# Top-k attention on one core: who negates the row maxima, and in which order TensorE takes scores, context and film products

## The chip, the cores and the metric

The kernel runs on one core of one Trainium2 chip. The metric is the device time of one execution in microseconds. Before the change it is 2488.77 us (median of 3 runs, 2488.7 to 2490.81). The engines are TensorE (PE, with its weight loads as PEld), VectorE (DVE), ScalarE (ACT), GpSimd (POOL) and SyncE (SP, which only issues transfers here). Each runs its own instruction list strictly in order, and semaphores tie the lists together.

## The reference, cut to what matters

The program is a decoder of two layers. The part that the change touches is the top-k attention of the second one, followed by an S4D convolution:

```
Q = (x_text @ Wq).reshape(B, T, H=4, DH=32);  K likewise from x_vision
scores = einsum('bthd,bghd->bhtg', Q, K) / sqrt(DH);  masked where vision_mask is false
topv, topi = top_k(scores, 32);  probs = softmax(topv)
attn = zeros.at[topi].set(probs);  attn_mean = attn.mean(axis=heads)
c_t = einsum('btg,bgd->btd', attn_mean, V) * text_mask
x = layernorm(x_text, g_norm_in, b_norm_in)
scale_in, shift_in   = split(c_t @ W_film_in  + b_film_in, 2)
x = x * (1 + gate * scale_in) + gate * shift_in
y = s4d(x, ...)
scale_out, shift_out = split(c_t @ W_film_out + b_film_out, 2)
y = y * (1 + gate * scale_out) + gate * shift_out
```

There are 2048 text rows, taken as 16 tiles of 128. A tile has 4 heads of 256 scores.

## The kernel before, in words

`topk_attention` (L2114 on) is one block with one hand-written instruction list for each engine. Nothing is scheduled automatically: the order of the Python calls is the order on the engine. Tile n goes through these steps.

- TensorE, `scores(n)`: four products of 32 rows (one a head) into the single buffer SC. ScalarE, `scale(n)`: copies SC to one of three buffers SS with the factor 1/sqrt(32). GpSimd, `mask(n)`: adds the mask to SS.
- VectorE: four rounds r = 0 to 3. Each finds the 8 greatest of each head (`max`, L2416) and strikes them out with `match_replace` (L2429), so that WW ends as the scores without the greatest 32. After round 0 `tensor_scalar` (L2435) writes NM, the negated maxima, and adds to `max_ready`. In round 0 of tile n stands also `inverse(n - 1)`: reciprocal and scaling of the sums of the tile before, which waits for `sums_ready`.
- ScalarE, in one turn n of its loop: `exp_left(n - 1)` (exp of WW), `diagonal(n - 1)` (four diagonal matrices of the inverse sums), `exp_all(n)` (exp of SS with the bias NM), `apply(n)` (layer norm of a row tile), `film(n - 2)` (copies out both film products), `turned_out(n - 1)`, `scale(n + 2)`, `pooled_out(n - 1)`, `sums(n)` (exp of the 32 found, with their sum).
- GpSimd: `selected(n)` subtracts WW from SS, which leaves only the 32 greatest, and adds to `probs_ready`.
- TensorE, `turn(n)`: multiplies SS by the diagonals, which turns the probabilities, weighs them and adds the heads up. `pool_context(n)`: the product with V. `film(n)`: two products of 512 columns with a bias row each, the first (in) and the second (out).

TensorE's loop before is, for one n: `scores(n + 2)`, `turn(n - 1)`, `pool_context(n - 1)`, `film(n - 1)` with both halves. At the stage's start it takes query groups 0 and 1, `scores(0)`, groups 2 and 3, `scores(1)`. VectorE first does the statistics of the layer norm of all 16 tiles, waits for the square root on ScalarE (`std_ready`), and then takes tile 0. The stage after this one (`s4d_convolve`) starts on TensorE once this block is finished.

Of the kernel before, what the change touches and what calls it, by code (L numbers as in the profile page):

```python
# [9 lines left out]
P = 128  # L10
B, S, D = 8, 256, 256
T = B * S
NT = T // P
KD = D // P
# [7 lines left out]
ALU = mybir.AluOpType  # L22
# [2097 lines left out]
def topk_attention(nc, io, X, XT, ident, CTT, Z, FO, conv_loads, inputs):  # L2120
# [5 lines left out]
    with Stage(nc, "tk") as st:  # L2126
# [37 lines left out]
        masked = st.sem("masked")  # L2164
        max_ready = st.sem("max_ready")
        found_ready = st.sem("found_ready")
# [16 lines left out]
        with st.block() as block:  # L2183
# [6 lines left out]
            def _(pe):  # L2190
# [36 lines left out]

                def film(n):
# [3 lines left out]
                    for i in range(2):  # L2232
                        if n:
                            pe.wait_ge(film_out_read if i else film_in_read, n)
                        for k in range(KD):
                            pe.matmul(FP[:, i, :], CTT[:, k, n * P:(n + 1) * P], WI[:, i, k, :], start=(k == 0), stop=False)  # L2236
                        add_bias(pe, ident, FP[:, i, :], BI[:, i, :]).then_inc(film_ready, 1)

                inputs.loads.wait(pe)
                queries(0)  # L2240
                queries(1)
                scores(0)
                queries(2)
                queries(3)
                scores(1)
                film_loads.wait(pe)
                for n in range(NT + 1):
                    if n + 2 < NT:
                        scores(n + 2)
                    if n:  # L2250
                        turn(n - 1)
                        pool_context(n - 1)
                        film(n - 1)

# [37 lines left out]
            def _(act):  # L2292
# [40 lines left out]
                def film(n):  # L2333
                    act.wait_ge(film_ready, 2 * n + 1)
                    if n >= 2:
                        act.wait_ge(updated, n - 1)
                    act.activation(FI[:, n % 2, 0:D], FP[:, 0, 0:D], ACT.Identity, scale=GATE[:], bias=ident[:, ONES:ONES + 1])
                    act.activation(FI[:, n % 2, D:2 * D], FP[:, 0, D:2 * D], ACT.Copy, scale=GATE[:]).then_inc(film_in_read, 1)
                    act.wait_ge(film_ready, 2 * n + 2)
                    act.activation(FO[:, n, :], FP[:, 1, :], ACT.Copy, scale=GATE[:]).then_inc(film_out_read, 1)  # L2340
# [8 lines left out]

                queries(0)  # L2350
                queries(1)
                scale(0)
                queries(2)
                queries(3)
                act.wait_ge(stats_ready, 1)
                act.activation(RS[:], MV[:, :, 1], ACT.Sqrt, bias=ident[:, EPS5:EPS5 + 1]).then_inc(std_ready, 1)
                scale(1)
                film_loads.wait(act)
                for n in range(NT + 2):
                    if 1 <= n <= NT:  # L2360
                        exp_left(n - 1)
                        diagonal(n - 1)
                    if n < NT:
                        exp_all(n)
                        apply(n)
                    if n >= 2:
                        film(n - 2)
                    if 1 <= n <= NT:
                        turned_out(n - 1)
                    if n + 2 < NT:  # L2370
                        scale(n + 2)
                    if 1 <= n <= NT:
                        pooled_out(n - 1)
                    if n < NT:
                        sums(n)

            @block.vector
            def _(v):
                ch = Chain(v, dve_chain)

                def norm_stats():
# [3 lines left out]
                    for t in range(NT):  # L2385
                        ins = v.bn_aggr(MV[:, t, :], raw[:, t, :])
                    ins.then_inc(stats_ready, 1)
                    v.wait_ge(stats_ready, 1)
                    v.wait_ge(std_ready, 1)
# [13 lines left out]
                for n in range(NT):  # L2403
# [5 lines left out]
                    for r in range(LAST + 1):  # L2409
                        src = ww if r else SS[:, n % RB]  # L2410
                        found = [0, 0]
                        for i, pair in enumerate(PAIRS):
                            if r:
                                ch.need(struck[i])
# [6 lines left out]
                        if r == 0 and n:  # L2421
                            inverse(n - 1)
                        for i, pair in enumerate(PAIRS):
                            if r == LAST and i:
# [5 lines left out]
                            if r == LAST and i:  # L2430
                                ins.then_inc(struck_ready, 1)
                            else:
# [923 lines left out]
```

## Time and profile before

| | us |
|---|---|
| median of 3 runs | 2488.77 |
| profiled execution, its own time | 2487.0 |
| its span | 2485.2 |
| TensorE busy, whole span | 2177.0 (88%) |
| VectorE busy, whole span | 1639.0 (66%) |
| ScalarE busy, whole span | 986.8 (40%) |
| first matmul of the top-k block | 1323.63 |
| VectorE's first search of a maximum | 1335.92 |
| first matmul of the convolution after it | 1557.14 |

So the block takes 233.5 us of the span. The shares of the whole program say little about it: other stages have other limits. In this block VectorE is busy nearly without a gap and TensorE has gaps in each tile, so the stage has to be read from the timeline of each engine, tile by tile. The execution's own time is 1.8 us above its span, and that goes with no stage.

### The profile page before, as it was taken

The numbers are of one execution on the slowest core, as the hardware profiler recorded it, in microseconds if no ns is written. First come the engines' busy times: TensorE is split into PE (matmuls) and PEld (weight loads), VectorE is DVE, ScalarE is ACT, GpSimd is POOL, SyncE is SP. The second block draws the span as 40 slices with busy tenths as digits, with TensorE's granted clock in tenths as the row PEclk, the third lists the DMA queues.
The fourth block names the chain that finished last, engine by engine and source line by source line (L and its number), as shares of the span: only waits on it lengthen the run. The fifth ranks groups of instructions, "written<-read, shape, count | busy, mean of one in ns | idle before, by whom it ended". The sixth has DMA issues, their size and how long they took to land. (4 is left out here: it accounts for less than half of the span.)

```text
span 2485.2 us, 34016 instructions
## 1 busy us (share of the span) xinstructions
PE 2177.0 (88%) x12318; PEld 1487.9 (60%) x12318; DVE 1639.0 (66%) x4179; ACT 986.8 (40%) x2077; POOL 889.1 (36%) x513
## 2 busy tenths in 40 slices
PE   8788888998996897699896888869888899999997
PEld 3355555633663897366474444336655788888886
DVE  6699999713656112546327997541479788888886
ACT  2498988512855331315424776032100312112210
POOL 0298888102532984214102655431401210111110
PEclk9899999999998899799998898979899999999998
DMA  3121111000005575300101000030030000000001
GB/s 102 44 81 47 51 48 51 2 11 0 1 1 193 207 239 174 101 1 2 58 0 41 1 1 1 1 117 0 1 136 1 3 1 1 1 1 1 1 1 34
DMA packets 63803, 109.34 MB, mean 44 GB/s; under 512 B 12498, under 2 KB 44115, under 8 KB 61973
## 3 DMA queue, kind: packets, MB, share of 16 engines
q1 hardware_dynamic: 62100, 102.98, 12.6%
q0 software_dynamic: 1536, 4.20, 0.5%
q8 instruction: 98, 1.61, 0.3%
q14 instruction: 69, 0.56, 0.1%
HBM read 94.19 MB, written 12.98 MB: 43 GB/s over the span
## 5 line engine op out<-in xcount | busy, mean ns | idle before, releaser
L749 POOL TENSOR_TENSOR XT<-mamba_DU,scan_BS 128x1024 f32<-128x1024 f32 x128 | 299.0, 2364 | 148.4 <-DMA scan_BS<-mamba_rows 110.8
L878 DVE TENSOR_TENSOR_SCAN scan_H<-scan_AB,XT 128x512 f32<-128x512 f32 x256 | 296.3, 1209 | 8.1 <-POOL XT L749 4.8
L3022 PE MATMUL ex_HP<-XT,pe_DOWN 128*128 128x256 f32 x1024 | 249.9, 391 | 6.3 <-PEq L2758 5.5
L3053 PE MATMUL ex_OP<-pe_UP,ex_GH 128*128 128x256 f32 x1024 | 231.5, 380 | 0.0
L3083 ACT ACTIVATE ex_GH<-ex_HP 128x512 f32<-128x512 f32 x128 | 76.4, 598 | 380.8 <-PE ex_HP L3022 346.1
L763 PEld LDWEIGHTS scan_TP<-ident,scan_H 128*128 128x128 f32 x1024 | 120.1, 142 | 157.2 <-DVE scan_H L878 81.2
L808 ACT ACTIVATE scan_AB<-mamba_E,mamba_AA 128x510 f32<-128x510 f32 x256 | 198.7, 776 | 37.9 <-DVE scan_H L878 33.5
L3022 PEld LDWEIGHTS ex_HP<-XT,pe_DOWN 128*128 128x128 f32 x1024 | 194.5, 195 | 31.9 <-issue 5.7
L3053 PEld LDWEIGHTS ex_OP<-pe_UP,ex_GH 128*128 128x128 f32 x1024 | 194.3, 190 | 25.9
L772 PE MATMUL scan_YT<-mamba_BC,ident 128*128 128x512 f32 x384 | 198.5, 599 | 4.1 <-ACT scan_YS L824 2.3
L763 PE MATMUL scan_TP<-ident,scan_H 128*128 128x128 f32 x1024 | 147.7, 278 | 45.8 <-DVE scan_H L878 45.8
L3109 POOL TENSOR_TENSOR ex_AS<-ex_AS,pe_IV 128x512 f16<-128x512 f16 x32 | 52.9, 1682 | 363.3 <-DVE ex_AS L3157 363.3
L3134 DVE TENSOR_TENSOR ex_L<-ex_IOTA,ex_KEYS 128x4096 f16<-128x4096 f16 x64 | 151.8, 2372 | 2.2
L817 ACT ACTIVATE mamba_BC<-scan_TP,scan_CT 128x512 f32<-128x512 f32 x192 | 129.3, 674 | 3.9 <-PE scan_TP L763 3.9
L3208 DVE SCALAR_TENSOR_TENSOR ex_GH<-ex_GP,ex_GH 128x1024 f32<-128x1024 f32 x64 | 78.4, 1225 | 61.0 <-issue 32.4
L1656 DVE TENSOR_SCALAR experts_HT<-experts_HP 128x320 f32<-128x320 f32 x32 | 15.7, 492 | 133.4 <-PE experts_HP L1593 133.4
L3042 PEld LDWEIGHTS ex_GP<-ex_R,ex_L 128*128 128x128 f16 x2048 | 77.8, 117 | 15.3 <-DVE ex_L L3134 4.5
L1608 PE MATMUL experts_YT<-experts_HT,moe_W 128*128 128x160 f32 x512 | 78.2, 314 | 8.0 <-ACT experts_HT L1624 7.5
L3042 PE MATMUL ex_GP<-ex_R,ex_L 128*128 128x32 f16 x2048 | 77.7, 191 | 7.2 <-DVE ex_L L3134 3.8
L2038 POOL TENSOR_TENSOR pfcore_A<-pfcore_A,pg_MASK 128x512 f32<-128x512 f32 x32 | 40.6, 1268 | 114.5 <-ACT pfcore_A L2018 114.5
L1608 PEld LDWEIGHTS experts_YT<-experts_HT,moe_W 128*128 128x128 f32 x512 | 74.7, 201 | 10.5 <-ACT experts_HT L1624 8.2
L2236 PE MATMUL tk_FP<-tk_WI,s_CTT 128*128 128x512 f32 x128 | 74.1, 708 | 7.6 <-ACT s_CTT L2348 7.6
(449 smaller groups left out, 4535.3 us busy)
## 6 DMA issues: line engine op xcount, KB each, us to landing
moe_W<-in_L_ffn_w SPq DMA_DIRECT2D x32, 1024.0 KB, 7.6
scan_BS<-mamba_rows SPq DMA_DIRECT2D x64, 256.0 KB, 3.2
pe_DOWN<-in_L_ffn_down SPq DMA_DIRECT2D x1, 4096.0 KB, 12.6
pe_UP<-in_L_ffn_up SPq DMA_DIRECT2D x1, 4096.0 KB, 22.7
moe_dispatch<-moe_BOTH SPq DMA_DIRECT2D x1, 2560.0 KB, 14.2
experts_XE<-moe_dispatch SPq DMA_DIRECT2D x16, 160.0 KB, 2.4
moe_answers<-experts_YE SPq DMA_DIRECT2D x16, 160.0 KB, 3.4
XT<-in_xT SPq DMA_DIRECT2D x4, 512.0 KB, 5.6
```

What stands on the lines that cost most here:

```text
L749: pool.tensor_tensor(BU[:, r % 2, cs], tokens(DU, cs, r // DS), row, ALU.mult).then_inc(bu_ready, 1)
L763: ins = pe.transpose(TP[:, i % SLOTS, c * P:(c + 1) * P], H[:, r % 2, c, tb * P:(tb + 1) * P], ident[:, 0:P])
L772: pe.matmul(YT[:, tb, :], ident[:, 0:P], HT[:, n % 4, :], start=(s == 0), stop=(s == DS - 1)).then_inc(y_added, 1)
L808: act.activation(later(AB[:, n % 2, :]), later(tokens(E, c, g)), ACT.Exp, scale=AA[:, 2 * c, s:s + 1], bias=AA[:, 2 * c, s:s + 1]).then_in ...
L817: act.activation(HT[:, n % 4, :], TP[:, item(r, tb) % SLOTS, :], ACT.Copy, scale=CT[:, TB * g + tb, s:s + 1]).then_inc(act_read, 1)
L878: v.tensor_tensor_scan(H[:, r % 2, c], AB[:, n % 2, :], BU[:, r % 2, c], 0.0, ALU.mult, ALU.add).then_inc(h_ready, 1)
L1608: ins = pe.matmul(YT[:, k * CAP:(k + 1) * CAP], W2[:, e % 2, c, k * P:(k + 1) * P], HT[:, e % 2, c, :], start=(c == 0), stop=(c == NHID - 1))
L3022: ins = pe.matmul(HP[:, n % 2, a, :], DOWN[:, k, 2 * q + a, :], XT[:, k, b * BLK:(b + 1) * BLK], start=(k == 0), stop=(k == KD - 1))
L3042: ins = pe.matmul(GP[:, n % 2, t, :], L[:, n % 2, t // RUN, :, t % RUN], R[:, n % 2, t // RUN, :, t % RUN], start=True, stop=True)
L3053: ins = pe.matmul(OP[:, m % 2, 0:D], GH[:, b % 2, j, a * P:(a + 1) * P], UP[:, j, :], start=(j == 0), stop=(j == J2 - 1))
L3134: v.tensor_tensor(L[:, n % 2], numbers(P), along(0, P), ALU.is_equal).then_inc(left_ready, 1)
L3208: v.scalar_tensor_tensor(gh, GP[:, n % 2].rearrange("p t j -> p j t"), 1.0 / PSCALE, gh, ALU.mult, ALU.mult).then_inc(gated, 1)
```

## The change

Three things change, all in `topk_attention`.

1. The negated maxima NM are made on ScalarE, at the head of `exp_all`, and not by VectorE. VectorE's last strike of round 0 now adds to `first_struck`; ScalarE waits for it, writes NM (128x4) with an activation, waits for its own write (`shift_ready`), and goes on with the exponentials.
2. At the start, `scores(0)` follows the first query group and `scores(1)` the third, and ScalarE's `scale(0)` and `scale(1)` move up with them. VectorE's reciprocal of the standard deviations moves from before tile 0 into round 1 of tile 0 (`norm_scale`).
3. In TensorE's loop the second film product of tile n - 2 stands between `turn(n - 1)` and `pool_context(n - 1)`, and `scores(n + 2)` behind `pool_context(n - 1)`; the first film product stays last. On ScalarE the copy of the second film product (`film_out`) moves behind `pooled_out(n - 1)`; `scale(n + 2)` stays in front of `pooled_out(n - 1)`.

```diff
+                def film(n, i):
                     pe.wait_ge(pooled_read, n + 1)
...
                 inputs.loads.wait(pe)
                 queries(0)
+                scores(0)
                 queries(1)
-                scores(0)
                 queries(2)
+                scores(1)
                 queries(3)
-                scores(1)
                 film_loads.wait(pe)
                 for n in range(NT + 1):
+                    if n:
+                        turn(n - 1)
+                    if n >= 2:
+                        film(n - 2, 1)
+                    if n:
+                        pool_context(n - 1)
                     if n + 2 < NT:
                         scores(n + 2)
                     if n:
-                        turn(n - 1)
-                        pool_context(n - 1)
-                        film(n - 1)
+                        film(n - 1, 0)
+                film(NT - 1, 1)
...
                 def exp_all(n):
-                    act.wait_ge(max_ready, n + 1)
+                    act.wait_ge(first_struck, n + 1)
+                    act.activation(NM[:, n % 2, :], MX[:, n % 2, :, 0], ACT.Copy, scale=-1.0).then_inc(shift_ready, 1)
+                    act.wait_ge(shift_ready, n + 1)
...
                         scale(n + 2)
                     if 1 <= n <= NT:
                         pooled_out(n - 1)
+                    if 2 <= n <= NT + 1:
+                        film_out(n - 2)
                     if n < NT:
                         sums(n)
...
                         if r == 0 and n:
                             inverse(n - 1)
+                        if r == 1 and n == 0:
+                            norm_scale()
...
-                        if r == 0:
-                            v.tensor_scalar(NM[:, n % 2, :], mx[:, :, 0], -1.0, None, ALU.mult).then_inc(max_ready, 1)
```

TensorE's list in the middle of the loop, before. tk_TP from tk_DG and tk_SS is `turn`, tk_TP from tk_AT and topk_V is `pool_context`, tk_FP with tk_WI and its row with tk_BI is one film product, tk_SC is `scores`:

```order
L2205 MATMUL tk_SC<-topk_KT,tk_QT 128x256 x4
L2216 MATMUL tk_TP<-tk_DG,tk_SS 128x128 x8
L2224 MATMUL tk_TP<-tk_AT,topk_V 128x128 x4
L2236 MATMUL tk_FP<-tk_WI,s_CTT 128x512 x2
L158 MATMUL tk_FP<-tk_BI,ident 128x512
L2236 MATMUL tk_FP<-tk_WI,s_CTT 128x512 x2
L158 MATMUL tk_FP<-tk_BI,ident 128x512
```

The same turn of the loop after the change:

```order
L2217 MATMUL tk_TP<-tk_DG,tk_SS 128x128 x8
L2236 MATMUL tk_FP<-tk_WI,s_CTT 128x512 x2
L158 MATMUL tk_FP<-tk_BI,ident 128x512
L2225 MATMUL tk_TP<-tk_AT,topk_V 128x128 x4
L2206 MATMUL tk_SC<-topk_KT,tk_QT 128x256 x4
L2236 MATMUL tk_FP<-tk_WI,s_CTT 128x512 x2
L158 MATMUL tk_FP<-tk_BI,ident 128x512
```

Between turning and context there was nothing, and now there is one film product; the scores stood ahead of the turning and now stand behind the context.

ScalarE's list in the middle of the loop, before. tk_AT is `turned_out`, tk_SS from tk_SC is `scale`, s_CTT is `pooled_out`, tk_FI and s_FO are the copies of the first and the second film product, tk_MJ is `sums`, tk_WW is `exp_left`:

```order
L2331 ACTIVATE s_Z<-X,tk_NB,tk_RS 128x256
L2337 ACTIVATE tk_FI<-tk_FP,ident,tk_GATE 128x256
L2338 ACTIVATE tk_FI<-tk_FP,tk_GATE 128x256
L2340 ACTIVATE s_FO<-tk_FP,tk_GATE 128x512
L2344 ACTIVATE tk_AT<-tk_TP 128x256
L2301 ACTIVATE tk_SS<-tk_SC 128x1024
L2348 ACTIVATE s_CTT<-tk_TP 128x2x128
L2311 ACTIVATE tk_MJ,tk_SM<-tk_MX,tk_NM 128x32 x4
L2317 ACTIVATE tk_WW<-tk_WW,tk_NM 128x256 x4
L2325 ACTIVATE tk_DG<-ident,tk_SM 128x128 x4
```

After the change:

```order
L2344 ACTIVATE tk_FI<-tk_FP,ident,tk_GATE 128x256
L2345 ACTIVATE tk_FI<-tk_FP,tk_GATE 128x256
L2353 ACTIVATE tk_AT<-tk_TP 128x256
L2306 ACTIVATE tk_SS<-tk_SC 128x1024
L2357 ACTIVATE s_CTT<-tk_TP 128x2x128
L2349 ACTIVATE s_FO<-tk_FP,tk_GATE 128x512
L2318 ACTIVATE tk_MJ,tk_SM<-tk_MX,tk_NM 128x32 x4
L2324 ACTIVATE tk_WW<-tk_WW,tk_NM 128x256 x4
L2332 ACTIVATE tk_DG<-ident,tk_SM 128x128 x4
L2310 ACTIVATE tk_NM<-tk_MX 128x4
```

The copy of the second film product moved from in front of tk_AT to behind s_CTT, and the write of tk_NM is new; the copy of the scores stands where it stood, one place ahead of s_CTT.

## Rows read from the trace of the kernel before

**Rows 1.** Windows: us, busy time (instructions) of PE, PEld, DVE, ACT, POOL, PEclk, DMA share, GB/s.

```profile
1340.00:1540.00 200.00, 159.26 (x638) 85.85 (x638) 199.48 (x799) 142.13 (x415) 110.52 (x91) 0.86 0.00 1
1391.00:1392.00 1.00, 1.00 (x8) 1.00 (x7) 1.00 (x5) 1.00 (x4) 0.86 (x2) 0.58 0.00 0
1400.00:1401.00 1.00, 1.00 (x2) 0.34 (x2) 0.97 (x6) 1.00 (x4) 0.08 (x1) 0.50 0.00 0
```

**Rows 2.** Timeline of VectorE, one tile: start us, us, instruction, [idle before it <-releaser].

```profile
1450.35 1.39 DVE L2416 MAX8 tk_MX<-tk_SS 128x8 f32<-128x256 f32 x4
...
1453.51 1.11 DVE L2435 TENSOR_SCALAR tk_NM<-tk_MX 128x4 f32<-128x4 f32 x1
1454.54 1.39 DVE L2416 MAX8 tk_MX<-tk_WW 128x8 f32<-128x256 f32 x4
...
1463.18 1.39 DVE L2416 MAX8 tk_MX<-tk_SS 128x8 f32<-128x256 f32 x4
```

**Rows 3.** Tile tk_NM: count, duration ns min/median/max, first and last start.

```profile
L2435 DVE TENSOR_SCALAR tk_NM<-tk_MX x16: 359/1110/1118, 1338.8 to 1530.5; 128x4 f32<-128x4 f32 x16
```

**Rows 4.** Timeline of GpSimd, the subtraction of the same tile.

```profile
1452.24 2.35 POOL L2270 TENSOR_TENSOR tk_SS<-tk_SS,tk_WW 128x1024 f32<-128x1024 f32 x1 [2.93 <-ACT tk_WW L2317]
```

**Rows 5.** Timeline of ScalarE, the same tile.

```profile
1450.46 1.70 ACT L2317 ACTIVATE tk_WW<-tk_WW,tk_NM 128x256 f32<-128x256 f32 x4 [0.24 <-DVE tk_WW L2429]
...
1454.66 1.71 ACT L2306 ACTIVATE tk_SS<-tk_SS,tk_NM 128x256 f32<-128x256 f32 x4 [1.32 <-DVE tk_NM L2435]
...
1457.57 0.67 ACT L2340 ACTIVATE s_FO<-tk_FP,tk_GATE 128x512 f32<-128x512 f32 x1
...
1458.40 1.02 ACT L2301 ACTIVATE tk_SS<-tk_SC 128x1024 f32<-128x1024 f32 x1
1459.90 0.38 ACT L2348 ACTIVATE s_CTT<-tk_TP 128x256 f32<-128x256 f32 x1 [0.48 <-PE tk_TP L2224]
1461.73 0.32 ACT L2311 ACTIVATE tk_MJ<-tk_MX,tk_NM 128x32 f32<-128x32 f32 x1 [1.44 <-DVE tk_MX L2416]
...
1462.87 0.19 ACT L2311 ACTIVATION_READ_ACCUMULATOR tk_MJ<-tk_MX,tk_NM 128x1 f32 x1
```

**Rows 6.** Timeline of TensorE, tiles in the middle and at the end.

```profile
1368.74 1.16 PE L2224 MATMUL tk_TP<-tk_AT,topk_V 128*128 128x128 f32 x8 [1.86 <-ACT tk_AT L2344]
1370.38 3.51 PE L2236 MATMUL tk_FP<-tk_WI,s_CTT 128*128 128x512 f32 x4 [0.47 <-ACT s_CTT L2348]
...
1454.65 2.05 PE L2216 MATMUL tk_TP<-tk_DG,tk_SS 128*128 128x128 f32 x16 [0.85 <-POOL tk_SS L2270]
...
1539.10 1.12 PE L158 MATMUL tk_FP<-tk_BI,ident 1*128 1x512 f32 x2
...
1542.07 1.12 PE L158 MATMUL tk_FP<-tk_BI,ident 1*128 1x512 f32 x2
1544.47 3.54 PE L2216 MATMUL tk_TP<-tk_DG,tk_SS 128*128 128x128 f32 x16 [1.28 <-POOL tk_SS L2270]
```

**Rows 7.** Timeline of TensorE, the first tiles.

```profile
1336.49 0.71 PE L2205 MATMUL tk_SC<-topk_KT,tk_QT 32*128 32x256 f32 x8 [1.24 <-ACT tk_SS L2301]
1343.79 1.24 PE L2205 MATMUL tk_SC<-topk_KT,tk_QT 32*128 32x256 f32 x8 [6.58 <-ACT tk_SS L2301]
1352.01 3.78 PE L2216 MATMUL tk_TP<-tk_DG,tk_SS 128*128 128x128 f32 x16 [6.99 <-POOL tk_SS L2270]
1356.26 1.51 PE L2224 MATMUL tk_TP<-tk_AT,topk_V 128*128 128x128 f32 x8 [0.47 <-ACT tk_AT L2344]
```

**Rows 8.** Timelines of ScalarE, GpSimd and VectorE, the stage's start.

```profile
1327.42 0.60 ACT L2295 ACTIVATE tk_QT<-tk_FP 128x512 f32<-128x512 f32 x1 [5.08 <-PE tk_FP L2195]
...
1331.04 1.02 ACT L2301 ACTIVATE tk_SS<-tk_SC 128x1024 f32<-128x1024 f32 x1
...
1332.22 2.35 POOL L2265 TENSOR_TENSOR tk_SS<-tk_SS,tk_MB 128x1024 f32<-128x1024 f32 x1 [8.18 <-ACT tk_SS L2301]
...
1335.92 1.40 DVE L2416 MAX8 tk_MX<-tk_SS 128x8 f32<-128x256 f32 x4
```

More of the change, by code:

```diff
@@ L2164, in topk_attention @@
         masked = st.sem("masked")
-        max_ready = st.sem("max_ready")
+        first_struck = st.sem("first_struck")
+        shift_ready = st.sem("shift_ready")
         found_ready = st.sem("found_ready")
@@ L2226, in pool_context @@
                     ins.then_inc(pooled, 1)
-                def film(n):
+                def film(n, i):
                     pe.wait_ge(pooled_read, n + 1)
@@ L2231, in film @@
                         pe.wait_ge(queries_read, T // G4)
[L2232 to L2237, printed above, removed]
+                    else:
+                        pe.wait_ge(film_out_read if i else film_in_read, n)
+                    for k in range(KD):
+                        pe.matmul(FP[:, i, :], CTT[:, k, n * P:(n + 1) * P], WI[:, i, k, :], start=(k == 0), stop=False)
+                    add_bias(pe, ident, FP[:, i, :], BI[:, i, :]).then_inc(film_ready, 1)
                 inputs.loads.wait(pe)
                 queries(0)
+                scores(0)
                 queries(1)
-                scores(0)
                 queries(2)
+                scores(1)
                 queries(3)
-                scores(1)
                 film_loads.wait(pe)
                 for n in range(NT + 1):
+                    if n:
[4 more added lines that the diff above has]
+                        pool_context(n - 1)
                     if n + 2 < NT:
@@ L2338, in film, with film_out @@
                     act.activation(FI[:, n % 2, D:2 * D], FP[:, 0, D:2 * D], ACT.Copy, scale=GATE[:]).then_inc(film_in_read, 1)
+                def film_out(n):
                     act.wait_ge(film_ready, 2 * n + 2)
@@ L2350, in _ @@
                 queries(0)
+                scale(0)
                 queries(1)
-                scale(0)
-                queries(2)
-                queries(3)
                 act.wait_ge(stats_ready, 1)
                 act.activation(RS[:], MV[:, :, 1], ACT.Sqrt, bias=ident[:, EPS5:EPS5 + 1]).then_inc(std_ready, 1)
+                queries(2)
                 scale(1)
+                queries(3)
                 film_loads.wait(act)
@@ L2387, in norm_stats, with norm_scale @@
                     ins.then_inc(stats_ready, 1)
+                def norm_scale():
                     v.wait_ge(stats_ready, 1)
@@ L2412, in _ @@
                         for i, pair in enumerate(PAIRS):
-                            if r:
+                            if r == 1 and i:
+                                v.wait_ge(first_struck, n + 1)
+                            elif r:
                                 ch.need(struck[i])
@@ L2431, in _ @@
                                 ins.then_inc(struck_ready, 1)
+                            elif r == 0 and i:
+                                ins.then_inc(first_struck, 1)
                             else:
                                 struck[i] = ch.mark(ins)
-                        if r == 0:
-                            v.tensor_scalar(NM[:, n % 2, :], mx[:, :, 0], -1.0, None, ALU.mult).then_inc(max_ready, 1)
                 inverse(NT - 1)
```

## The prediction, made before the changed kernel had run

> **What bounds the kernel now.** I read the windows first, then the timeline of each engine over one tile, last the tile of the negated maxima.
>
> The windows say who is full: in 200 us of the loop VectorE is busy for 199.48, TensorE for 159.26, ScalarE for 142.13, GpSimd for 110.52 [rows 1]. VectorE has no gap, so its work per tile is the period: from the first search of one tile to that of the next 1463.18 - 1450.35 = 12.83 us [rows 2]. The others wait for it: ScalarE stands idle 1.44 us before the sums and 1.32 us before the exponentials [rows 5].
>
> One VectorE row is odd. The write of NM has 4 elements a row and takes 1.11 us at the median, but 0.36 at least [rows 3]. In the tile shown it starts at 1453.51 and ends at 1454.62 [rows 2]; GpSimd's subtraction runs from 1452.24 to 1454.59 [rows 4]. So it stands until GpSimd is done. It costs VectorE 1454.54 - 1453.51 = 1.03 us a tile.
>
> The Trainium skill says the same ("SBUF — State Buffer", section "Who interferes with whom"): a VectorE instruction in a two-port mode and a GpSimd instruction exclude each other for their whole length, and `tensor_scalar` can be one. The end times above agree. The same section says that a VectorE instruction with two SBUF inputs waits for a GpSimd instruction that reads SBUF. Of what is left in VectorE's loop that is the scaling in `inverse`; nothing on the path below waits for it before 1.6 us later.
>
> **VectorE's side of the change.** It loses 1.03 us in each of 15 tiles and about 0.27 in the first (0.36 less the overlap of 0.09 that other rows show). Its own need falls to 12.83 - 1.03 = 11.80 us a tile. If VectorE stayed the bound, that is 15 x 1.03 = 15.4 us gained.
>
> **ScalarE's side.** It gets an activation of 4 elements and a wait for it. The trace has no such pair; the nearest rows are the 0.19 and 0.32 us of reading a sum and of the exponential of 32 elements [rows 5]. Bounds: 0.2 without any latency to 0.6 with a round trip; I take 0.35. Queued behind it are the exponentials, the norm and the first film copies, then the copy of the turned tile. Before, that copy starts 1458.40 - 0.27 = 1458.13, 7.67 us behind `exp_left` (1450.46), with 1.32 of waiting and 0.57 of the moved film copy in it [rows 5]. Now: 7.67 - 1.32 - 0.57 + 0.35 = 6.1 us. TensorE has turned the tile 6.1 to 6.2 us behind `exp_left` (below) and then does 2.97 us of film, so the 0.35 is covered by some 2.6 us and costs nothing.
>
> **TensorE's order, the step that decides.** Follow what now stands between `exp_left(n - 1)` and `exp_left(n)` on ScalarE. The context comes only after the film product. The scores of tile n + 2 come only after the context. ScalarE's `scale(n + 2)` waits for those scores and stands in front of `pooled_out`, `film_out` and `sums(n)`, and `exp_left(n)` stands behind them. That is a closed ring through three engines, once a tile. With TensorE at its full level (2.4 GHz), each term from one start to the next, an engine's overlap of 0.1 us with its successor taken off:
>
> - `exp_left` to GpSimd's start: 1452.24 - 1450.46 = 1.78 [rows 4, 5]
> - subtraction to the first turning matmul: 1454.65 - 1452.24 = 2.41 [rows 4, 6]
> - turning: 2.05 - 0.1 = 1.95 [rows 6]
> - second film product: 1542.07 - 1539.10 = 2.97 (one half with its bias) [rows 6]
> - context: 1.16 - 0.1 = 1.06 [rows 6]
> - scores, and on to ScalarE: 0.71 + 0.04 = 0.75 [rows 7]
> - `scale`: 1.02 - 0.09 = 0.93; `pooled_out`: 0.38 - 0.1 = 0.28; `film_out`: 0.67 - 0.1 = 0.57 [rows 5]
> - `sums`: 1462.87 + 0.19 - 1461.73 = 1.33, less 0.1: 1.23 [rows 5]
>
> Sum: 13.93 us. That is 2.1 above VectorE's new 11.80 and 1.1 above the 12.83 of before. In the old order neither the film product nor the scores lay in it, and ScalarE waited 1.44 us for VectorE before the sums: the ring was slack. Now VectorE waits in `inverse(n - 1)` for the sums, some 2 us a tile, and its saving goes there.
>
> **The clock.** TensorE's share of the ring is 1.95 + 2.97 + 1.06 + 0.71 = 6.69 us and would double at the half level (1.2 GHz), so the ring lies between 13.93 and 20.6. The mean granted clock over the loop is 0.86 [rows 1]. It fell behind waits: after 1.86 and 0.47 us of waiting the film product took 3.51 us, four matmuls that take 2.97 - 1.05 = 1.92 at the full level; after 1.28 us the last turning took 3.54 instead of 2.05 [rows 6]. One such stretch still stood at 0.50 at 1400, having begun in the microsecond after 1391 (0.58) [rows 1]. Before, VectorE hid all that. In the new order TensorE ends its first film product at 12.13 + 0.15 + 2.97 = 15.25 us behind `exp_left(n - 1)` and turns next at 13.93 + 1.78 + 2.41 = 18.1: a wait of 2.9 us before every turning, longer than the waits that I quote from the loop. So I charge the 1.5 us of a slow turning to every tile, and the 1.6 us of a slow film product to about one in three (0.5): 13.93 + 2.0 = 15.9 us a tile. That is nearer to the full level, since the low stretches mostly last for one or two groups.
>
> **Start.** Before, VectorE's first search starts at 1335.92, 1.35 us after the mask of tile 0 (1332.22 + 2.35), since it waits for the square root behind all four query copies [rows 8]. Now: query group 0 copied at 1327.42 + 0.60 = 1328.02 [rows 8]; scores at the half level 1.24 and the hop 0.1: 1329.35 [rows 7]; `scale` and hop as before, 1332.22 - 1331.04 = 1.18; mask 2.35 [rows 8]; VectorE at about 1332.95. Gain 2.97. The norm's two small instructions, now in round 1 of tile 0, cost between 0.2 and the 0.7 of two undisturbed NM rows [rows 3]; I take 0.4. NM gives 0.27 back. Net -2.85 at `exp_left(0)`.
>
> **First and last tiles.** The first step has no second film product and follows a long wait, as before, when turning, context and scores took 3.78, 1.51 and 1.24 [rows 7]: 1.78 + 2.41 + 3.68 + 0.43 + 1.41 + 1.28 + 0.93 + 0.28 + 1.23 = 13.4. Then twelve full steps of 15.9 make 190.8. The last two have no scores and no `scale` (-1.68): 2 x 14.2 = 28.4. Together 232.6, against 15 x 12.83 = 192.5: +40.1. Behind the last `exp_left` one film product (2.97) now stands where TensorE waited 0.47 us: +2.5 (the slow turning is already in before [rows 6]).
>
> **Sum.** -2.85 + 40.1 + 2.5 = +39.8 us on the profiled 2487.0, that is 2526.8. The median of before is 1.8 above its profiled run; so **2529 us**.
>
> **Rivals.**
>
> A. *The ring holds, TensorE keeps its full level.* Now the film product fills the old wait of 1.86 us ahead of the context [rows 6], TensorE works 6.7 us in one piece, and that could hold the clock up. Then twelve steps of 13.93 (167.2), two of 12.25 (24.5) and the first 13.4 make 205.1, +12.6; with -2.85 and +2.5 less 1.5 for the last turning: +10.8, 2500 us. The Trainium skill ("TensorE: Matmul & The Clock Gate", section "What's actually happening") says that the low clock is the default and that activity lifts it, which is this rival's reason. Against it: the work is not more, only denser, and the wait before the turning grows to 2.9.
>
> B. *TensorE stays low for most of the time.* A longer period means less work in the same time, and a slower matmul lengthens the period again. At 18 us a step: 12 x 2.1 = 25 more, 2554 us. For it: ten microseconds in one piece at the half level [rows 1]. Against: at the half level TensorE has almost no waits left, and a mean of 0.86 [rows 1] means that it was low for only 28% of the time even with the old waits.
>
> C. *Faster: VectorE stays the bound.* Its mechanism is NM: 15.4 us of standing behind GpSimd is gone, and the ring fits beneath 11.80 us. With the start: 2489 - 15.4 - 2.85 + 1 = 2472 us. It decides if the ring is 2.1 us shorter than my sum at the full clock. For it: each term is taken from one tile. Against: every term is a row, no two of them can run side by side on one engine's list, and only the slow clock can move the sum, upward.
>
> D. *The change nets out.* The ring costs little more than 12.83 and the start pays it back. That needs 13.0 us, which no row gives.
>
> **Chances and range.** Forecast (2515 to 2543 as its own range) 0.74; A 0.10; B 0.08; C 0.06; D 0.02. For 8 in 10 I leave out C, D and the upper half of B: 2498 to 2546. A measurement of this kernel tells 0.2% (5 us) from no change: faster 0.06, same 0.03, slower 0.91.
>
> **What would show it.** Right: in the changed profile VectorE has a gap of 2 to 4 us in each tile before the reciprocal in `inverse`, released by ScalarE's sums; ScalarE waits in `scale` for TensorE's scores; the period between two `exp_left` is 14 to 17 us; context starts right behind the film's bias row; the NM row on ScalarE is below 0.4 us; the first search starts near 1333. Wrong: VectorE without gaps and a period of 11.8 (C), a period of 13.9 with the clock near 1 (A), or a lasting 0.5 (B). If ScalarE waits longest for something else than the scores or the context, my ring is not the one that decides.

## The result, and the profile after

| | before | after |
|---|---|---|
| median | 2488.73 us (2488.15 to 2490.81, 4 runs) | 2522.38 us (2518.95 to 2523.85, 4 runs) |
| profiled execution, its own time | 2487.0 | 2518.95 |
| its span | 2485.2 | 2517.1 |
| the top-k block, first matmul to first matmul of the convolution | 233.5 | 263.8 |

The change makes the kernel slower: the ratio is 1.0131 (95% interval 1.0115 to 1.0147), +33.65 us by the medians. The forecast was 2529, with a range of 2498 to 2546. Of the 31.9 us by which the two profiled spans differ, 30.3 lie in the block, 1.1 before it and 0.5 behind it.

First the windows of the kernel after, 140 us of the loop. The columns are those of [rows 1].

```profile
1360.00:1500.00 140.00, 100.34 (x398) 55.41 (x396) 110.09 (x463) 86.40 (x261) 72.17 (x60) 0.89 0.00 1
```

VectorE had no gap before [rows 1]. Now it is busy for 110.09 of 140 us: the engine that set the period stands idle for a fifth of the time, and no other engine is fuller. So the bound is not an engine but a chain of waits through several. The longest waits of three engines in the block, after, 1340 to 1575 (who waits on which tile, who releases it: total us, count, longest):

```profile
ACT tk_SS L2306 <- PE tk_SC L2206: 59.6, 13, 5.4
PE tk_TP L2217 <- POOL tk_SS L2275: 54.0, 16, 13.0
DVE tk_SM L2408 <- ACT tk_MJ L2318: 45.1, 15, 4.2
```

The first two lie on the ring: ScalarE waits in `scale` for the scores (59.6 / 13 = 4.6 us each), and TensorE waits for the subtraction before it turns a tile (one of these waits, of 13.0 us, is that of the first tile). The third shows that VectorE stands outside it with time to spare: it waits in `inverse` for ScalarE's sums (45.1 / 15 = 3.0 us each). One tile at TensorE's full level, first ScalarE:

```profile
1451.63 1.70 ACT L2324 ACTIVATE tk_WW<-tk_WW,tk_NM 128x256 f32<-128x256 f32 x4
...
1454.39 0.20 ACT L2310 ACTIVATE tk_NM<-tk_MX 128x4 f32<-128x4 f32 x1
1454.63 1.71 ACT L2313 ACTIVATE tk_SS<-tk_SS,tk_NM 128x256 f32<-128x256 f32 x4
...
1457.90 0.38 ACT L2353 ACTIVATE tk_AT<-tk_TP 128x256 f32<-128x256 f32 x1 [0.26 <-PE tk_TP L2217]
1462.43 1.02 ACT L2306 ACTIVATE tk_SS<-tk_SC 128x1024 f32<-128x1024 f32 x1 [4.15 <-PE tk_SC L2206]
1463.35 0.38 ACT L2357 ACTIVATE s_CTT<-tk_TP 128x256 f32<-128x256 f32 x1
1463.62 0.69 ACT L2349 ACTIVATE s_FO<-tk_FP,tk_GATE 128x512 f32<-128x512 f32 x1
1464.18 0.33 ACT L2318 ACTIVATE tk_MJ<-tk_MX,tk_NM 128x32 f32<-128x32 f32 x1
...
1465.40 1.70 ACT L2324 ACTIVATE tk_WW<-tk_WW,tk_NM 128x256 f32<-128x256 f32 x4
```

TensorE, from the turn of the loop before to the next, the tile before this one and a late one:

```profile
1440.58 3.51 PE L2217 MATMUL tk_TP<-tk_DG,tk_SS 128*128 128x128 f32 x16 [2.77 <-POOL tk_SS L2275]
1443.92 1.88 PE L2236 MATMUL tk_FP<-tk_WI,s_CTT 128*128 128x512 f32 x4
...
1455.81 2.05 PE L2217 MATMUL tk_TP<-tk_DG,tk_SS 128*128 128x128 f32 x16 [2.77 <-POOL tk_SS L2275]
1457.70 1.88 PE L2236 MATMUL tk_FP<-tk_WI,s_CTT 128*128 128x512 f32 x4
1459.51 1.12 PE L158 MATMUL tk_FP<-tk_BI,ident 1*128 1x512 f32 x2
1460.56 1.16 PE L2225 MATMUL tk_TP<-tk_AT,topk_V 128*128 128x128 f32 x8
1461.65 0.71 PE L2206 MATMUL tk_SC<-topk_KT,tk_QT 32*128 32x256 f32 x8
1463.78 1.98 PE L2236 MATMUL tk_FP<-tk_WI,s_CTT 128*128 128x512 f32 x4 [1.42 <-ACT s_CTT L2357]
...
1469.59 2.56 PE L2217 MATMUL tk_TP<-tk_DG,tk_SS 128*128 128x128 f32 x16 [2.77 <-POOL tk_SS L2275]
1471.93 3.10 PE L2236 MATMUL tk_FP<-tk_WI,s_CTT 128*128 128x512 f32 x4
```

VectorE in the same tile, two firsts of a search and what waits between them:

```profile
1447.10 1.40 DVE L2431 MAX8 tk_MX<-tk_SS 128x8 f32<-128x256 f32 x4
...
1451.77 0.18 DVE L2408 RECIPROCAL tk_SM<-tk_SM 128x4 f32<-128x4 f32 x1 [3.27 <-ACT tk_MJ L2318]
...
1462.28 1.39 DVE L2431 MAX8 tk_MX<-tk_SS 128x8 f32<-128x256 f32 x4
```

Follow the ring from `exp_left` at 1451.63 to the next at 1465.40: 4.18 us to the turning (1455.81), 1.89 to the film product, 2.86 to the context, 1.09 to the scores, 0.78 to `scale`, 0.92 to `pooled_out`, 0.27 to `film_out`, 0.56 to `sums`, 1.22 to `exp_left`. That is 13.77 us, and each term starts when the one before it ends. The wait of 2.77 us before nearly every turning is new (0.85 and 1.28 in [rows 6]), and behind it the turning mostly takes 3.51 us instead of 2.05, or 2.56 with a film product of 3.10 instead of 1.88. That it is the clock, the windows over these groups say: the turning of 3.51, that of 2.05, that of 2.56 and the film product of 3.10 behind it (columns as in [rows 1], PEclk is the third from the end).

```profile
1440.58:1443.92 3.34, 3.34 (x16) 3.34 (x17) 3.34 (x17) 1.82 (x5) 2.66 (x4) 0.54 0.03 5
1455.81:1457.70 1.89, 1.89 (x17) 1.89 (x17) 1.89 (x8) 1.83 (x5) 1.36 (x2) 1.00 0.00 0
1469.59:1471.93 2.34, 2.34 (x16) 2.34 (x17) 2.34 (x11) 1.82 (x5) 1.74 (x3) 0.79 0.00 0
1471.93:1474.97 3.04, 3.04 (x6) 1.02 (x5) 3.04 (x14) 0.38 (x1) 1.07 (x2) 0.60 0.01 3
```

The granted clock is 0.54 over the slow turning and 1.00 over the fast one; in the third case it falls within the turning (0.79) and stays low into the film product (0.60).

### The profile page after: what moved, and what is told of

It is laid out like the page before. It is cut to its first block and busy times, and to the rows that moved or that the text cites. A ratio compares the mean times of both kernels' runs of the same rounds, so it can differ in the third digit from the quotient of the medians.

```text
span 2517.1 us, 34032 instructions
## 1 busy us (share of the span) xinstructions
PE 2179.8 (87%) x12318; PEld 1492.7 (59%) x12318; DVE 1625.8 (65%) x4163; ACT 986.9 (39%) x2093; POOL 889.0 (35%) x513
## 3 DMA queue, kind: packets, MB, share of 16 engines
q1 hardware_dynamic: 62100, 102.98, 12.2%
q8 instruction: 99, 1.62, 0.3%
## 5 line engine op out<-in xcount | busy, mean ns | idle before, releaser
L1656 DVE TENSOR_SCALAR experts_HT<-experts_HP 128x320 f32<-128x320 f32 x32 | 15.7, 492 | 133.1 <-PE experts_HP L1593 133.1
L2217 PE MATMUL tk_TP<-tk_DG,tk_SS 128*128 128x128 f32 x256 | 50.0, 375 | 54.0 <-POOL tk_SS L2275 54.0
L3059 PEld LDWEIGHTS ex_GP<-ex_R,ex_L 128*128 128x128 f16 x2048 | 77.9, 117 | 15.2 <-DVE ex_L L3151 4.5
L2217 PEld LDWEIGHTS tk_TP<-tk_DG,tk_SS 128*128 128x128 f32 x256 | 46.2, 279 | 66.8 <-POOL tk_SS L2275 66.8
```

What stands on the lines that cost most here:

```text
L2217: ins = pe.matmul(TP[:, n % 2, 0, k * P:(k + 1) * P], SS[:, n % RB, h, k * P:(k + 1) * P], DG[:, h, :], start=(h == 0), stop=(h == XH - 1))
L3059: ins = pe.matmul(GP[:, n % 2, t, :], L[:, n % 2, t // RUN, :, t % RUN], R[:, n % 2, t // RUN, :, t % RUN], start=True, stop=True)
```

## The experiments

All times of the block are taken in the same way from each trace, in us: "start" from the first query matmul to `exp_left(0)`; "steps" the fifteen periods between two `exp_left`; "typical step" the one that most full tiles have; "tail" from the last `exp_left` to the convolution's first matmul.

| kernel | start | steps | typical step | tail | block | median | ratio to before (95%) |
|---|---|---|---|---|---|---|---|
| before | 24.2 | 192.5 | 12.83 | 16.9 | 233.5 | 2488.7 | |
| after | 20.4 | 224.3 | 15.2 to 15.5 | 19.1 | 263.8 | 2522.4 | 1.0131 (1.0115 to 1.0147) |
| x1, scores in front again | 20.4 | 203.8 | 13.66 | 19.1 | 243.3 | 2501.8 | 1.005 (1.0034 to 1.0067) |
| x2, film back | 20.4 | 178.1 | 11.68 | 15.4 | 213.9 | 2473.3 | 0.9935 (0.9918 to 0.9951) |
| x3, both back | 20.4 | 177.1 | 11.81 | 15.4 | 212.9 | 2472.0 | 0.9933 (0.9917 to 0.995) |
| x4, NM back on VectorE | 21.7 | 221.8 | 15.2 to 15.5 | 19.2 | 262.7 | 2518.5 | 1.0124 (1.0107 to 1.0141) |
| x5, after + film twice | 22.8 | 207.2 | 13.78 | 21.0 | 251.0 | 2506.0 | 1.0068 (1.0051 to 1.0085) |
| x6, before + NM on ScalarE | 22.3 | 177.1 | 11.81 | 16.7 | 216.1 | 2474.1 | 0.9942 (0.9925 to 0.9959) |
| x7, before + new start | 21.6 | 192.5 | 12.83 | 15.7 | 229.8 | 2487.8 | 0.9998 (0.9988 to 1.0007) |
| x8, after + `scale` late | 20.4 | 226.5 | 14.7 and 16.0 | 19.3 | 266.2 | 2522.7 | 1.0138 (1.0121 to 1.0155) |
| x9, x1 + film twice | 22.8 | 182.6 | 12.20 | 21.0 | 226.4 | 2482.5 | 0.9974 (0.9953 to 0.9995) |

The block's times come from one profiled execution of each kernel, the medians from all of them. The part of the span ahead of the block differs between these executions by up to 13.5 us (x8 reaches the block at 1337.09, before at 1323.63, with the same code up to there), so a difference of a few us is safer read from the block.

### x1: the scores ahead of the turning again

```diff
                 for n in range(NT + 1):
+                    if n + 2 < NT:
+                        scores(n + 2)
                     if n:
                         turn(n - 1)
                     if n >= 2:
                         film(n - 2, 1)
                     if n:
                         pool_context(n - 1)
-                    if n + 2 < NT:
-                        scores(n + 2)
```

> The changed kernel with one thing undone: the scores of tile n + 2 stand ahead of the turning again; the second film product stays in front of the context. Ring theory: the ring loses the scores (0.75 us), and scale (0.92) runs beside the film product, so a step is 13.77 - 1.67 = 12.1 us at TensorE's full level. One slow turning (1.5) in most tiles: 12.2 to 13.7 a step, against 15.3 in the changed kernel and 12.83 before. With the start's gain (3.8) and the tail's loss (2.2): about 2500 us, 2492 to 2508. ScalarE no longer waits for scores. Rival 'the film product in front of the context is the whole loss': the time stays within 5 us of the changed kernel (2517 to 2527). Rival 'only the scores are': the time falls to VectorE's 11.8 a step, 2470 us.

Measured: 2501.8, as the ring has it. TensorE of x1 in its loop:

```profile
1462.31 3.52 PE L2217 MATMUL tk_TP<-tk_DG,tk_SS 128*128 128x128 f32 x16 [2.34 <-POOL tk_SS L2274]
1465.67 1.88 PE L2236 MATMUL tk_FP<-tk_WI,s_CTT 128*128 128x512 f32 x4
...
1468.53 1.16 PE L2225 MATMUL tk_TP<-tk_AT,topk_V 128*128 128x128 f32 x8
```

and ScalarE:

```profile
1469.73 0.38 ACT L2356 ACTIVATE s_CTT<-tk_TP 128x256 f32<-128x256 f32 x1 [2.56 <-PE tk_TP L2225]
```

With the scores out of the ring, ScalarE waits for the context alone. From the context's start to `pooled_out` it is now 1469.73 - 1468.53 = 1.20 us, where after needs 1.09 to the scores, 0.78 to `scale` and 0.92 to `pooled_out`: 1.59 less. Twelve full steps fall from 15.31 to 13.73 on the mean, which is 19.0 us, and the first step by 1.5; the two kernels' times differ by 20.6. The period that is left, 13.66, is 12.2 and one slow turning (3.52 instead of 2.05). The late scores alone therefore don't explain the loss: 29.8 of the 50.4 us by which after stands behind x3 remain.

### x2: the second film product back behind the first

```diff
                     if n:
                         turn(n - 1)
-                    if n >= 2:
-                        film(n - 2, 1)
-                    if n:
                         pool_context(n - 1)
                     if n + 2 < NT:
                         scores(n + 2)
                     if n:
                         film(n - 1, 0)
-                film(NT - 1, 1)
+                        film(n - 1, 1)
```

> The changed kernel with the other thing undone: both film products of tile n - 1 stand behind the scores again, and the context follows the turning; scores stay behind the context, ScalarE's order is unchanged. Ring theory: the ring loses the film product (2.86), but then ScalarE's own work (copy of the turned tile 6.1 us behind exp_left) sets the context: 6.1 + 0.43 + 1.08 + 0.78 + 0.92 + 0.27 + 0.56 + 1.22 = 11.4 us at the full level, below VectorE's 11.8. TensorE has 9.7 us of work in it; slow stretches lift the step to 12 to 13: about 2494 us, 2478 to 2502. Rival 'only the film product is the loss': 2470 us. Rival 'the scores are the whole loss': within 5 us of the changed kernel.

Measured: 2473.3, below the expected 2478 to 2502, a miss in the good direction. I had expected slow stretches of TensorE and a ring near VectorE's need. TensorE, x2:

```profile
1390.68 2.05 PE L2217 MATMUL tk_TP<-tk_DG,tk_SS 128*128 128x128 f32 x16
1393.20 1.16 PE L2225 MATMUL tk_TP<-tk_AT,topk_V 128*128 128x128 f32 x8 [0.47 <-ACT tk_AT L2350]
1394.29 0.71 PE L2206 MATMUL tk_SC<-topk_KT,tk_QT 32*128 32x256 f32 x8
1396.43 1.98 PE L2236 MATMUL tk_FP<-tk_WI,s_CTT 128*128 128x512 f32 x4 [1.42 <-ACT s_CTT L2354]
...
1402.36 2.05 PE L2217 MATMUL tk_TP<-tk_DG,tk_SS 128*128 128x128 f32 x16
```

ScalarE in the same tile:

```profile
1395.07 1.02 ACT L2303 ACTIVATE tk_SS<-tk_SC 128x1024 f32<-128x1024 f32 x1 [1.92 <-PE tk_SC L2206]
1395.99 0.38 ACT L2354 ACTIVATE s_CTT<-tk_TP 128x256 f32<-128x256 f32 x1
```

and the windows of x2:

```profile
1360.00:1500.00 140.00, 117.18 (x524) 60.97 (x528) 139.22 (x591) 112.07 (x335) 93.36 (x78) 1.00 0.00 1
```

The turning starts without a wait and takes 2.05; thirteen turnings in a row do (the first took 3.78, and a late one, behind 1.62 us of waiting, 3.49), and the mean granted clock is 1.00. VectorE is nearly full again. Without the film product the ring through `exp_left` is slack, but the late scores make another one, along TensorE's own list. One turning starts at 1390.68 and the next at 1402.36: 2.52 us to the context, 1.09 to the scores, 0.78 to `scale`, 0.92 to `pooled_out`, 0.44 to the first film product, and 5.93 for both film products. That is 11.68, the step of seven tiles in the middle, in which ScalarE catches up what it lost in the first two (13.31 and 12.25). It is just below VectorE's 11.81, at which the last six steps run. So the late scores, with the late copy of the second film product, cost next to nothing by themselves (x2 stands 1.3 us behind x3, which its interval does not tell from nothing), and the late scores cost 20.6 us once the film product is in the ring too.

### x3: TensorE's loop and the film copy as before

```diff
                 for n in range(NT + 1):
+                    if n + 2 < NT:
+                        scores(n + 2)
                     if n:
                         turn(n - 1)
-                    if n >= 2:
-                        film(n - 2, 1)
-                    if n:
                         pool_context(n - 1)
-                    if n + 2 < NT:
-                        scores(n + 2)
-                    if n:
                         film(n - 1, 0)
-                film(NT - 1, 1)
+                        film(n - 1, 1)
...
                     if n >= 2:
                         film(n - 2)
+                        film_out(n - 2)
```

> The changed kernel with TensorE's loop and ScalarE's copy of the second film product as before the change; the negation on ScalarE and the new start stay. Ring theory: the ring is slack, VectorE is the bound with 11.80 us a step: 15 x 1.03 = 15.4, and the start gives 3 to 4: 2470 us, 2467 to 2473. Rival 'the negation on ScalarE costs what it saves on VectorE': 2485 us or more. Rival 'TensorE becomes the bound once a step is 11.8' (10.3 us of work, more in slow stretches): 2475 to 2483.

Measured: 2472.0 (2471.64 to 2472.36), 0.9933 of before: this is the version that beats both. What stays of the change is NM on ScalarE and the new start. TensorE, x3:

```profile
1446.26 2.05 PE L2217 MATMUL tk_TP<-tk_DG,tk_SS 128*128 128x128 f32 x16 [0.63 <-POOL tk_SS L2271]
1449.37 1.16 PE L2225 MATMUL tk_TP<-tk_AT,topk_V 128*128 128x128 f32 x8 [1.07 <-ACT tk_AT L2349]
```

and its windows:

```profile
1360.00:1500.00 140.00, 115.72 (x529) 62.00 (x528) 139.59 (x595) 113.41 (x330) 93.34 (x78) 1.00 0.00 1
```

VectorE is busy for 139.59 of 140 us and the step is 11.81, VectorE's own need as the prediction had it (11.80). The clock is at 1.00. In the kernel before the same stretch reads:

```profile
1360.00:1500.00 140.00, 118.54 (x484) 63.65 (x484) 139.62 (x556) 102.01 (x293) 84.82 (x72) 0.89 0.00 1
```

So with the period 1 us shorter there are no falls of the clock in this stretch: the same work comes with 1 us less of waiting a tile.

### x5: the first film product twice

The theory of the slow matmuls was the weakest part of the sum, since it rests on which waits are long. This kernel adds work to TensorE where after waits: the first film product's matmuls (four in the profile, two calls in the code) run twice, with the same result.

```diff
                     else:
                         pe.wait_ge(film_out_read if i else film_in_read, n)
+                    if i == 0:
+                        for k in range(KD):
+                            pe.matmul(FP[:, i, :], CTT[:, k, n * P:(n + 1) * P], WI[:, i, k, :], start=(k == 0), stop=(k == KD - 1))
```

> The changed kernel with more work: the first film product's four matmuls of 512 columns run twice (the second pass overwrites the first, the result is the same), 1.91 us a tile inside the 2.77 us that TensorE waits before each turning. Clock theory (slow turnings come from the wait before them): the wait shrinks to about 0.9 us, most turnings take 2.05 and not 3.5, a step falls from 15.3 towards 13.8: 2500 to 2512 us, faster than the changed kernel although TensorE does 31 us more. Rival 'the clock falls for another reason': no gain, 2520 to 2526; rival 'the added work lies on the ring': up to 2550.

Measured: 2506.0. Sixteen times four matmuls more, and 16.4 us less than after. TensorE, x5:

```profile
1449.82 2.05 PE L2217 MATMUL tk_TP<-tk_DG,tk_SS 128*128 128x128 f32 x16 [1.06 <-POOL tk_SS L2278]
1451.70 1.88 PE L2239 MATMUL tk_FP<-tk_WI,s_CTT 128*128 128x512 f32 x4
```

and its windows:

```profile
1360.00:1500.00 140.00, 116.38 (x480) 59.80 (x480) 121.03 (x507) 92.19 (x279) 77.69 (x65) 0.98 0.00 1
```

The wait before the turning shrank from 2.77 to 1.06, the turning is back at 2.05 in most tiles, the mean clock at 0.98 instead of 0.89, and the step at 13.78, which is the ring's 13.77. The clock still fell now and then: behind the same 1.06 us two turnings of the loop took 3.13 and 2.47, with steps of 15.4, and the last two 3.03 and 3.20. The twelve full steps of after are 15.31 on the mean, so the clock's part of a step is 15.31 - 13.77 = 1.54 us. The added work and the shorter wait come together here, so this run shows that the clock is what the ring's sum leaves out, but not whether the clock goes by the length of that one wait or by how much TensorE works in all. The extra matmuls stand late enough in the tile that nothing in the ring waits for them; in the tail, where they end the chain, they cost 1.9 us. The start is 2.4 us longer too, ahead of the first of the extra matmuls: its scores took 1.24 us and not 0.71, and the norm's scaling stood behind GpSimd (last section). Why TensorE was slower there in x5 and x9 no run tells.

### x9: both, the scores in front and the film twice

> Scores ahead of the turning again, and the first film product's four matmuls run twice (same result, 1.91 us more work a tile). Its parent with the scores in front took 13.66 us a step: 12.18 of ring at the full level and 1.5 for a turning at the half level behind 2.34 us of waiting. Theory (the ring's terms add up, and the rest is the clock behind the wait): the wait shrinks to about 0.4 to 0.9 us at 12.2 a step, turnings take 2.05, a step is 12.2 to 12.6: 2484 to 2492 us, 10 to 18 below the parent's 2501.8 with 31 us more work on TensorE. Rival 'the 1.5 is not the clock but something else in the ring': 13.66 a step, 2502 to 2505.

This is the edit of x1 and that of x5 together. Measured: 2482.5, 1.5 us under the expected range, and 0.9974 of before by means, in which one execution of before at 2509.5 counts; by medians it is 4.2 us below the 2486.7 of before beside it. After a first step of 11.81 all steps are 12.20, each to 0.01. TensorE, x9:

```profile
1450.36 2.05 PE L2217 MATMUL tk_TP<-tk_DG,tk_SS 128*128 128x128 f32 x16 [0.64 <-POOL tk_SS L2277]
```

x1 to x9 is 19.3 us gained by 64 matmuls that change nothing (16.9 us in the block of the two traces: 21.2 in the steps, less 4.3 in start and tail); the ring without the scores is 12.2, as x1's 13.66 less a slow turning had said.

### x8: `scale` behind the film copy

```diff
                     if 1 <= n <= NT:
                         turned_out(n - 1)
-                    if n + 2 < NT:
-                        scale(n + 2)
                     if 1 <= n <= NT:
                         pooled_out(n - 1)
                     if 2 <= n <= NT + 1:
                         film_out(n - 2)
+                    if n + 2 < NT:
+                        scale(n + 2)
```

> The changed kernel with scale(n + 2) on ScalarE moved behind film_out(n - 2), so that pooled_out no longer waits for the scores; TensorE's order is the changed one. Ring theory: the scores' 0.75 us leave the ring (they run beside pooled_out and film_out), scale's 0.92 stays: 13.0 us a step at the full level. But TensorE then starts its first film product earlier and waits longer before the turning (some 3.6 us and not 2.8), so a slow turning in every tile, and more slow film products: 14.5 to 15.3 a step, 2510 to 2522 us. Rival 'ScalarE standing in scale with pooled_out behind it is the cause of the loss': 2490 or less.

Measured: 2522.7, just above the expected range and no different from after. At the full level the ring is 13.10 us now, 0.67 less, since `pooled_out` no longer stands behind the scores, but the time comes back. TensorE, x8:

```profile
1467.10 3.78 PE L2217 MATMUL tk_TP<-tk_DG,tk_SS 128*128 128x128 f32 x16 [3.58 <-POOL tk_SS L2275]
1470.68 3.09 PE L2236 MATMUL tk_FP<-tk_WI,s_CTT 128*128 128x512 f32 x4
```

TensorE's first film product starts and ends earlier, so the wait before the turning is 3.58 instead of 2.77. Now the turning is slow in every full tile (3.5 to 3.8), and in every second one the film product behind it too (3.09). The twelve full steps are 15.38 on the mean, so the clock's part grew from 1.54 to 2.3 us. The profiled execution itself took 2531.7, 9 us more than the other three: it came to the block 12 us later than after did, and its block is 2.4 us longer. I had the ring's sign right and its price in the clock too small.

### x4, x6 and x7: the other two parts by themselves

x4 puts NM back on VectorE in the kernel after:

```diff
-                    act.activation(NM[:, n % 2, :], MX[:, n % 2, :, 0], ACT.Copy, scale=-1.0).then_inc(shift_ready, 1)
                     act.wait_ge(shift_ready, n + 1)
...
+                        if r == 0:
+                            v.tensor_scalar(NM[:, n % 2, :], mx[:, :, 0], -1.0, None, ALU.mult).then_inc(shift_ready, 1)
```

> The changed kernel with the negation back on VectorE (after the last strike of round 0), everything else as changed. Ring theory: VectorE waits 1.9 to 4 us a tile for the sums, so it does not matter what it does in that tile: within 3 us of the changed kernel, 2519 to 2525, although the negation stands there until GpSimd's subtraction is done (about 2 us each, since it now starts right after GpSimd's). Rival 'the negation counts anywhere': 15 us and more slower than the changed kernel, 2537 or more.

Measured: 2518.5. VectorE's write now takes 2 us of standing (tile tk_NM of x4; columns as in [rows 3]):

```profile
L2452 DVE TENSOR_SCALAR tk_NM<-tk_MX x16: 1103/2071/2141, 1339.1 to 1559.4; 128x4 f32<-128x4 f32 x16
```

That is a microsecond more than before [rows 3] at the median, and the kernel is not slower for it (3.9 us faster by the medians, with intervals that overlap): the ring leaves VectorE 3 us of waiting. A saving on an engine that waits is worth nothing. Only the start is longer, by 1.2 us.

x6 is the kernel before with NM on ScalarE alone, and x7 the kernel before with the new start alone; both edits are those of the change's diff.

> The kernel before with only the negation moved to ScalarE. Theory: VectorE is the bound there, each step falls from 12.83 to 11.80 us: 15.4 + 0.3 us gained, 2473 us (2471 to 2476). Rival 'it is VectorE's own cost of a small instruction, not standing behind GpSimd': 0.27 x 16 = 4.3 us, 2484. Rival 'the round trip on ScalarE eats it': 2486 to 2490.

> The kernel before with only the new start (first scores behind the first query product, norm's reciprocal in round 1 of tile 0). Theory: the first search comes 3 to 4 us earlier and the loop is untouched: 2485.5 us (2484.5 to 2487.5). Rival 'the start is given back later': 2488 to 2489.

Measured: x6 2474.1, with a step of 11.81; the fifteen steps are 192.5 - 177.1 = 15.4 us shorter, as the prediction's 15 x 1.03. Its start is 1.9 us shorter as well, of which 1.6 is not the edit: the first two query groups, the same code, took TensorE 5.09 us and not the 6.70 of before. x7 2487.8, which its interval does not tell from before; it is 0.3 us above the expected range and below the rival's 2488, so the time decides between neither. In the profile its start is 2.6 us shorter and the block 3.7. The start alone brings less than in x3 since NM is still on VectorE there and stands behind the mask of tile 1. VectorE and GpSimd, x7, two timelines:

```profile
1337.49 1.30 DVE L2439 TENSOR_SCALAR tk_NM<-tk_MX 128x4 f32<-128x4 f32 x1
...
1336.42 2.35 POOL L2265 TENSOR_TENSOR tk_SS<-tk_SS,tk_MB 128x1024 f32<-128x1024 f32 x1 [1.85 <-ACT tk_SS L2301]
```

The one ends at 1338.79, the other at 1338.77; in before the same write took 0.36 us [rows 3].

## Why the prediction was right, point by point

- **The ring.** Right. Forecast 13.93 us with the clock at its full level; measured 13.77 in the tile above, 13.78 in x5. Every term is within 0.1 of its row but the film product (2.86 instead of 2.97). The order of the waits is the forecast one: scores before `scale`, sums before `inverse`. Taking the scores out (x1) shortens the ring by 1.59, where the prediction's last two steps took 1.68; taking the film product out (x2) leaves VectorE's 11.81 as the bound, with TensorE's own list at 11.68 just beside it.
- **The clock's charge.** That slow groups stand behind the new wait was right, the size too large, and this is most of the miss: 2.0 us a full tile forecast, 1.54 measured. The prediction added a slow film product in one tile of three to a slow turning in all. In fact the slow stretch mostly lasts for about one group: in ten of twelve full tiles either the turning takes 3.5 and the film product 1.88, or the turning 2.5 and the film product 3.1. In the first of the twelve both were slow (3.78 and 3.04, a step of 16.61), and in one neither. Twelve times 15.31 is 183.7 against 190.8. The last two steps were 13.66 each, not 14.2. That the length of the wait decides is not shown: before had turnings of 3.32 and of 2.05 behind the same 0.85 us.
- **VectorE's saving.** Right, and spent: 1.03 us a tile (x6), worth nothing under the ring (x4). Rival C named 2472 for the case that VectorE stays the bound; x2 (2473.3) and x3 (2472.0) are that case, which is reached only when the film product is out of the ring.
- **ScalarE's write of NM.** Right: 0.20 us at the median, hidden in ScalarE's wait for the turned tile (0.26 us in the tile above, 1.72 in the one before). The pair with its own wait is 0.24 from one start to the next (1454.39 to 1454.63), where I took 0.35.
- **The start.** Forecast -2.85, measured 24.19 - 20.42 = 3.77 less. The rows below are TensorE's start, after. The scores start 4.06 us behind the first query matmul, where I had 4.49, and they take 0.71 and not the 1.24 of the half level. These 0.96 us account for the difference, and they are TensorE's speed in the first groups, not the change: the prediction had taken the half level for the scores and before's time for the query group. That they came out faster is luck, since in before, x5 and x9, the first query groups were slower. The four kernels x1 to x3 and x8 have the same start (20.4).

```profile
1324.75 3.37 PE L2196 MATMUL tk_FP<-XT,topk_WQ 128*128 128x512 f32 x4 [1.71 <-PEq L3271]
1328.81 0.71 PE L2206 MATMUL tk_SC<-topk_KT,tk_QT 32*128 32x256 f32 x8 [0.69 <-ACT tk_QT L2300]
```

- **First step and tail.** 13.4 forecast, 13.33 measured, with the context at 1.76 and the scores at 0.71 where the prediction took 1.51 and 1.24, so in part by luck; +2.5 forecast, 19.05 - 16.85 = +2.2 measured.
- **The sum.** -3.77 + 31.87 + 2.2 = +30.3 us in the block against the forecast +39.8: 8.2 of the difference of 9.5 are the steps, and of these about 6 the clock and the rest the ring's 13.93 instead of 13.77. The medians hide a third of it: 1.6 us were lost outside the block, for which the forecast had nothing, and the median of after lies 3.4 us above its profiled execution and not the 1.8 that I had added, so the forecast of 2529 missed the 2522.4 by less than its sum missed the block.
- **The rivals.** A (the ring with the clock held, 2500) did not come about by the change, but x5 nearly makes it: 2506, of which 4.3 are the longer start and tail and 3.3 the two steps that were still slow. B (lasting half level) did not come: the mean clock is 0.89 in the loop.

What stays open: why the slow turnings alternate between 3.5 and 2.5 us behind the same wait of 2.77, and why one of them took 2.05. No run tells it. Nor does one separate the length of the wait from the amount of TensorE's work in a turn: x5 and x9 change both at once.

## What to carry to other kernels

When work is put in front of something on an in-order engine, don't ask whether that engine has room, but whether the work now stands in a closed ring through the other engines; add up one turn of the ring from start to start and compare it with the fullest engine's need. What two moves cost doesn't add up: here 1.3 us (the scores late) and 29.8 (the film product early) apart, 50.4 together, because a longer ring costs nothing only while it stays below VectorE's 11.8. And here the longer ring was paid twice, since it made TensorE wait and its clock was lower behind these waits (1.54 us a tile).

## What the hardware showed beside that

- **Small VectorE instructions stood behind GpSimd to its end.** The write of 128x4 took 0.36 us alone and 1.11 [rows 3], 1.30 (x7) and 2.07 (x4) behind a running GpSimd instruction. It held for an instruction with two inputs too: the norm's scaling of 128x16, 0.17 us alone in before, in x5 (VectorE and GpSimd, two timelines):

```profile
1339.78 1.69 DVE L2407 SCALAR_TENSOR_TENSOR tk_NB<-tk_MV,tk_RS 128x16 f32<-128x16 f32 x1
...
1339.10 2.34 POOL L2273 TENSOR_TENSOR tk_SS<-tk_SS,tk_MB 128x1024 f32<-128x1024 f32 x1 [3.83 <-ACT tk_SS L2309]
```

  They end 0.03 us apart (1341.47 and 1341.44). The Trainium skill ("SBUF — State Buffer", section "Who interferes with whom") has both kinds: a `tensor_scalar` can run in a mode that takes two ports, an instruction with two SBUF inputs contends with a GpSimd instruction that reads SBUF, and the one that comes second stands until the other is done. The end times here agree. I had charged 0.2 to 0.7 us for the norm's two instructions in round 1 of tile 0.
- **More matmuls made the kernel faster.** With 2.34 us of waiting before it the turning took 3.3 to 3.7 us (x1), with 3.58 it took 3.5 to 3.8 (x8), with 2.77 it took 3.4 to 3.5 in eight tiles, 2.5 in five and 2.05 in one (after). With 0.64 or none it took 2.05 (x9, x2), and with 1.06 it did so in most tiles (x5), though TensorE's work was the same or more. The Trainium skill ("TensorE: Matmul & The Clock Gate", section "What's actually happening") has the low clock as the default that activity lifts; x5 and x9, with more activity, agree, by 16.4 and 19.3 us.
- **The mean clock can hide it.** Over 1360 to 1500 it is 0.89 both before and after. But before, VectorE's need covered the slow matmuls (each step was 12.83), and after, they lie in the ring and cost 1.54 us a tile.
